# Second attention of a two-layer block: chunks of 512 tokens, parts copied inside SBUF, maxima added by a selection product

## What is computed

```python
qkv = (x @ W_qkv).reshape(B, S, 3, H, Dh)            # H = 16 heads of Dh = 8
q, k, v = (q[:, :, m], k[:, :, m], v[:, :, m])       # m: a fixed permutation of the tokens
qs = q.reshape(B, H, nseg, seg, Dh)                  # segments of 128 tokens
ks = k.reshape(B, H, nseg, seg, Dh)[:, :, :, ::dil]  # every second key: 64 per segment
scores = jnp.einsum('bhnqd,bhnkd->bhnqk', qs, ks) * scale
attn = jax.nn.softmax(scores, axis=-1)
out = jnp.einsum('bhnqk,bhnkd->bhnqd', attn, vs)
```

## Time and profile before

| | |
|---|---|
| median of three runs | 799.55 us |
| the profiled execution, its own time | 806.35 us |
| its span, first to last instruction | 804.5 us |
| mean granted TensorE clock | 0.915 |
| first attention, first to last unit | about 28.6 to 372 us |
| second attention, first `seg_max` to last weighted sum | 422.4 to 480.9 us |
| expert work begins | 522.4 us |

### The profile page before, as it was taken

One profiled execution on the slowest core, in us unless ns is written; L12 is line 12 of the kernel. 1 busy time (PEld: TensorE's weight loads), 2 busy tenths in 40 slices (PEclk: granted clock), 3 DMA queues, 4 the chain that ended last, 5 costly groups with the idle time before them and its releaser, 6 DMA issues.

```text
span 804.5 us, 16665 instructions
## 1 busy us (share of the span) xinstructions
PE 689.3 (86%) x5878; PEld 441.6 (55%) x5878; DVE 636.0 (79%) x1149; ACT 445.1 (55%) x974; POOL 155.7 (19%) x287
## 2 busy tenths in 40 slices
PE   7499888888888888899955988499999998998883
PEld 5233333333333333335533766499999997996652
DVE  2688999999999999942574647889999994554996
ACT  3058999999999999984641436202111114454442
POOL 6400000000000000003331007601111122123563
PEclk9558999999999999999985669589999998999998
DMA  7711111111111110002556500000000000000000
GB/s 197 222 22 32 32 32 31 32 32 31 33 31 32 32 31 3 2 3 68 142 140 172 156 16 1 0 1 0 2 0 0 0 0 1 0 0 1 15 13 26
DMA packets 19401, 31.87 MB, mean 40 GB/s; under 512 B 4952, under 2 KB 12504, under 8 KB 18040
## 3 DMA queue, kind: packets, MB, share of 16 engines
q1 hardware_dynamic: 17992, 29.42, 13.9%
q0 software_dynamic: 1344, 1.58, 0.7%
HBM read 23.25 MB, written 7.34 MB: 38 GB/s over the span
## 4 chain that ended last, share of the span: by engine, by line
PE 52%; ACT 18%; issue 10%; DVE 10%; DMA 5%; SPq 2%; POOL 2%; DVEq 0%; POOLq 0%; ACTq 0%
ACT probs L1166 16%; PE ps_hi L749 13%; PE ps_lo L998 7%; PE ps_lo L1000 6%; PE ps_lo L999 6%; PE ps_hi L763 4%; PE ps_hi L1058 3%; DMA q_rep<-mrow 2%; DVE probs L1747 2%; DVE mx L1465 2%; PE ps_hi L1049 1%; SPq L385 1%; ACT mrow L1121 1%; PE ps_hi L810 1%; PE ps_hi L930 1%
## 5 line engine op out<-in xcount | busy, mean ns | idle before, releaser
L1465 DVE TENSOR_REDUCE mx<-ps_lo 128x2 f32<-128x1024 f32 x256 | 306.2, 1224 | 12.2 <-PE ps_lo L726 9.0
L1166 ACT ACTIVATE probs<-ps_hi 128x512 f32<-128x512 f32 x512 | 278.0, 596 | 38.4 <-PE ps_hi L749 25.8
L763 PE MATMUL ps_hi<-probs,v_blk 128*32 128x256 f32 x2048 | 168.2, 401 | 5.6 <-ACT mrow L1121 5.5
L749 PE MATMUL ps_hi<-q,k 28*128 28x512 f32 x512 | 132.0, 509 | 26.9 <-ACT probs L1166 13.0
L726 PE MATMUL ps_lo<-k,q 26*128 26x512 f32 x512 | 135.7, 526 | 7.0 <-DVE mx L1465 4.2
L1681 DVE SCALAR_TENSOR_TENSOR tok_cur<-ps_lo,w_cur,tok_cur 128x384 f32<-128x384 f32 x240 | 127.6, 608 | 6.3 <-PE ps_lo L1000 4.7
L749 PEld LDWEIGHTS ps_hi<-q,k 28*128 28x128 f32 x512 | 49.5, 187 | 139.5 <-ACT probs L1166 117.7
L998 PE MATMUL ps_lo<-w_hi,op_hi 128*128 128x384 f32 (+1 forms) x304 | 108.1, 356 | 19.8 <-DVEq L1642 10.1
L999 PE MATMUL ps_lo<-w_lo,op_hi 128*128 128x384 f32 (+1 forms) x304 | 105.4, 347 | 0.0
L1000 PE MATMUL ps_lo<-w_hi,op_lo 128*128 128x384 f32 (+1 forms) x304 | 105.4, 347 | 0.0
L763 PEld LDWEIGHTS ps_hi<-probs,v_blk 128*32 128x32 f32 x2048 | 42.3, 109 | 72.5 <-ACT probs L1166 58.5
(11 more groups left out here) (225 smaller groups left out, 842.8 us busy)
## 6 DMA issues: line engine op xcount, KB each, us to landing
q<-q_parts SPq DMA_DIRECT2D x30, 192.0 KB
q_rep<-q_parts SPq DMA_DIRECT2D x8, 576.0 KB
k<-k_parts SPq DMA_DIRECT2D x32, 96.0 KB
k_rep<-k_parts SPq DMA_DIRECT2D x24, 96.0 KB
q_parts<-qk_hi SPq DMA_DIRECT2D x8, 256.0 KB, 4.9
q_parts<-qk_p SPq DMA_DIRECT2D x12, 128.0 KB, 3.1
xa<-in_L_attn_x SPq DMA_DIRECT2D x4, 256.0 KB, 3.9
q_parts<-qk_lo SPq DMA_DIRECT2D x4, 256.0 KB, 6.3
```

The costliest lines, as they stand in the source:

```text
L749: mm = pe.matmul(bank(4 + (2 * n + a) % 3), k0[rows, k_at:k_at + P], q0[rows, h * QN:(h + 1) * QN], start=True, stop=True)
L763: mm = pe.matmul(o_bank()[32 * r:32 * r + 32, 0:OW], v_all[:, at:at + 32], probs0[:, n % P_RING, r * OW:(r + 1) * OW], start=(kb == 0), st ...
L1166: act.activation(probs0[:, n % P_RING, a * QN:(a + 1) * QN], bank(4 + (2 * n + a) % 3), ACT.Exp).then_inc(s0_free, 1)
L1465: dve.reduce_max(mx2[:, j % 2, :, i, kh], bank(2 * (m % 2), 2).rearrange("p (a n) -> p a n", a=2), AX_X).then_inc(max0_done, 1)
```

## The change

Work is ordered by chunk instead of by batch entry: a step is now one chunk of 512 tokens (four segments) and eight of the sixteen heads, in two row strips of 64 partitions, one for even and one for odd heads. Only six pairs of parts are kept, 48 rows per strip, without the pairs (1, 2), (2, 1) and (2, 2). The way through DRAM goes: SyncE copies q (`load_q1`) and GpSimd copies k (`load_k1`) straight from the split parts, 12 DMAs each per chunk, 96 in all. For this the channels of q and k must lie in another order, which is made by permuting the weights: they are loaded into a staging tile and GpSimd copies them into place, at the start of the program, ahead of its work for head 0. The maxima are no longer two rows of q: after each head's four score products two products with a constant 0/1 matrix (`sel_sb`, 256 KB, loaded with the weights) add them. `seg_rows` gets a second product, `seg_o` moves from VectorE to ScalarE, and the transposes back are two per tile.

```diff
-ROWS = PARTS * PARTS * DH
+PART_PAIRS = ((0, 0), (0, 1), (0, 2), (1, 0), (1, 1), (2, 0))
+ROWS = len(PART_PAIRS) * DH
+HALF = 64
+HP = H // 2
+KN = QN // 2
...
-    dq1 = nc.dram_tensor("q_parts_1", [PARTS * DH, NH, S], BF16).ap()
-    dk1 = nc.dram_tensor("k_parts_1", [PARTS * DH, NH, S // 2], BF16).ap()
...
+        w_stage = attT[:, 0, 0:2 * D]
+        def copies_of(part, side):
+            return [i for i, pair in enumerate(PART_PAIRS) if pair[side] == part]
+        def copy_rows(strip, i):
+            return slice(HALF * strip + i, HALF * strip + ROWS, len(PART_PAIRS))
...
-            def store_q1(q):
...
-            def stored1(b):
...
-            def load_rep(s):
-                slot, n = s % RING, S * HG // 2
-                sp.dma_start(q_rep[0:ROWS, slot * HG * S:(slot + 1) * HG * S],
-                             dq1[:, s * HG:(s + 1) * HG].rearrange("r h n -> r (h n)").unsqueeze(1).broadcast_to(
-                                 [PARTS * DH, PARTS, HG * S])).then_inc(rep1_in[slot], 16)
...
-            def load_mrow(s):
-                at = (s % RING) * (HG * S)
-                sp.wait_ge(mrow_set, s + 1)
-                for part in range(2):
-                    dst = q_rep[MAX_ROW + part:MAX_ROW + part + 1, at:at + HG * S]
-                    sp.dma_start(dst.rearrange("o (r n) -> o r n", n=P), mrow[:, part, :]).then_inc(mrow_in, 16)
+            def load_q1(q):
+                for part in range(PARTS):
+                    sp.wait_ge(part_set[part], q + 1)
+                    for i in copies_of(part, 0):
+                        for strip in range(2):
+                            sp.dma_start(q_rep[copy_rows(strip, i), q * HP * QN:(q + 1) * HP * QN]
+                                         .rearrange("d (h n) -> d h n", n=QN),
+                                         qk_p[HALF * strip:HALF * (strip + 1), q, part, 0:QN]).then_inc(q1_in[q], 16)
...
-            for dst, src in ((wo_sb, wo), (w_qkv1, w_qkv), (wout_sb, w_out), (sim_sb, sim), (rank_sb, rank)):
+            for dst, src in ((wo_sb, wo), (wout_sb, w_out), (sim_sb, sim), (rank_sb, rank)):
                 sp.dma_start(dst[:], src).then_inc(ld_w1, 16)
+            sp.dma_start(w_qkv1[:, 2 * D:W3], w_qkv[:, 2 * D:W3]).then_inc(ld_w1, 16)
+            sp.dma_start(w_stage, w_qkv[:, 0:2 * D]).then_inc(ld_w1, 16)
+            sp.dma_start(sel_sb[:], sel).then_inc(ld_w1, 16)
...
-            for q in range(2):
-                store_q1(q)
-            stored1(0)
-            sp.wait_ge(const_set, 12)
+            sp.wait_ge(const_set, 11)
             sp.wait_ge(s0_ps, NU)
-            for s in range(2):
-                load_rep(s)
-            for q in range(2, NQ):
-                store_q1(q)
-            load_mrow(0)
-            for s in range(2, RING):
-                load_rep(s)
-            load_mrow(1)
-            stored1(1)
-            for s in range(NS - RING):
-                sp.wait_ge(seg_s_ps, 2 * (s + 1))
-                load_rep(s + RING)
-                load_mrow(s + 2)
-            for s in range(NS - RING + 2, NS):
-                load_mrow(s)
+            for q in range(NQ):
+                load_q1(q)
...
+            def load_k1(q):
+                for part in range(PARTS):
+                    pool.wait_ge(part_set[part], q + 1)
+                    for i in copies_of(part, 1):
+                        for strip in range(2):
+                            pool.dma_start(k_rep1[copy_rows(strip, i), q * HP * KN:(q + 1) * HP * KN]
+                                           .rearrange("d (h n) -> d h n", n=KN),
+                                           qk_p[HALF * strip:HALF * (strip + 1), q, part, QN:QN + KN]
+                                           ).then_inc(k1_in[q], 16)
...
+            pool.wait_ge(ld_w1, 7 * 16)
+            for n in range(2):
+                at = slice(n * D, (n + 1) * D)
+                pool.tensor_copy(w_qkv1[:, at].rearrange("p (s d h) -> p h s d", s=2, d=DH),
+                                 w_stage[:, at].rearrange("p (h s d) -> p h s d", s=2, d=DH)).then_inc(w1_set, 1)
...
-            fill(k_rep1[64:96, :].bitcast(words), two_ones)
...
-                for g in range(G):
-                    mm = pe.transpose(bank(t % 8)[:, g * P:(g + 1) * P], source(t, g), ident_sb[:])
+                for f in range(2):
+                    mm = pe.transpose(bank(t % 8)[:, f * P:(f + 1) * P], source(t, f), ident_sb[:])
...
+            def seg_at(s, h, g):
+                at = (s // 2 * HP + s % 2 * HG + h) * QUAD + g
+                return slice(at * SEG, (at + 1) * SEG), slice(at * KSEG, (at + 1) * KSEG)
+            def seg_max(s, step):
+                n = s * (HG + 2) + step
                 if n >= 2:
-                    pe.wait_ge(seg_max_done, n - (h > 0))
...
+                    pe.wait_ge(seg_max_done, n - (step > 0))
+                rows = slice(HALF * (step % 2), HALF * (step % 2) + ROWS)
+                for h in range(2):
+                    for g in range(QUAD):
+                        q_at, k_at = seg_at(s, step // 2 * 2 + h, g)
+                        c = (h * QUAD + g) * KSEG
+                        mm = pe.matmul(bank(step % 2)[:, c:c + KSEG], q_rep[rows, q_at], k_rep1[rows, k_at],
+                                       start=True, stop=True)
                 mm.then_inc(seg_max_ps, 1)
             def seg_rows(s):
                 pe.wait_ge(seg_max_all, s + 1)
-                pe.transpose(bank(0)[0:STEPS, 0:P], mx[:], ident_sb[:]).then_inc(seg_max_ps, 2)
+                pe.transpose(bank(0)[0:STEPS, 0:P], mx[:], ident_sb[:])
+                pe.matmul(bank(0)[STEPS:2 * STEPS, 0:P], mx[:], ident_sb[:], start=True, stop=True,
+                          tile_position=(0, STEPS)).then_inc(seg_max_ps, 2)
             def seg_scores(s, f):
-                slot = s % RING
-                pe.wait_ge(mrow_in, 32 * (s + 1))
+                pe.wait_ge(mrow_set, s + 1)
                 if s:
                     pe.wait_ge(seg_s_free, 2 * s - 1 + f)
-                for g in range(4 * f, 4 * f + 4):
-                    for h in range(HG):
...
+                for h in range(HG):
+                    def dst(u):
+                        return bank(2 + 2 * f, 2)[:, (u * HG + h) * SEG:(u * HG + h + 1) * SEG]
+                    for u, strip in ((0, 0), (1, 1), (1, 0), (0, 1)):
+                        q_at, k_at = seg_at(s, h, 2 * f + u)
+                        rows = slice(HALF * strip, HALF * strip + ROWS)
+                        pe.matmul(dst(u)[HALF * strip:HALF * (strip + 1)], k_rep1[rows, k_at], q_rep[rows, q_at],
+                                  start=True, stop=True, tile_position=(HALF * strip, HALF * strip))
+                    for u in range(2):
+                        at = ((2 * f + u) * HG + h) * P
+                        mm = pe.matmul(dst(u), sel_sb[:, at:at + P], mrow[:, s % 2, :], start=False, stop=True,
+                                       skip_group_check=True)
                 mm.then_inc(seg_s_ps, 1)
             def seg_out(s):
...
                 pe.wait_ge(seg_s_free, 2 * s + 2)
                 if s >= 2:
                     pe.wait_ge(seg_o_free, s - 1)
...
+                for g in range(QUAD):
+                    for h in range(HG):
+                        at = (s % 2) * 2 * S + (g * HG + h) * SEG
+                        mm = pe.matmul(bank(6 + s % 2)[32 * h:32 * h + 32, g * SEG:(g + 1) * SEG],
+                                       vblk(s // 2 * QUAD + g, s % 2 * HG + h), probs[:, 0, at:at + SEG],
+                                       start=True, stop=True, tile_position=(0, 32 * h))
...
-                pe.wait_ge(rep1_in[s % RING], (1 + PARTS) * 16 * (s // RING + 1))
+                if s % 2 == 0:
+                    pe.wait_ge(q1_in[s // 2], 2 * len(PART_PAIRS) * 16)
+                    pe.wait_ge(k1_in[s // 2], 2 * len(PART_PAIRS) * 16)
...
+            def seg_o(s):
+                act.wait_ge(seg_p_free, s + 1)
+                copy(o_seg[:, s * QN:(s + 1) * QN], bank(6 + s % 2)).then_inc(seg_o_free, 1)
...
-                if s:
-                    dve.wait_ge(mrow_in, 32 * s)
-                dve.tensor_scalar(mrow[:, 0, :], bank(0)[0:STEPS, 0:P], -1.0, None, ALU.mult).then_inc(seg_max_done, 1)
+                if s >= 2:
+                    dve.wait_ge(seg_s_ps, 2 * (s - 1))
+                low = slice(STEPS, 2 * STEPS)
+                dve.tensor_scalar(mrow[:, s % 2, :], bank(0)[0:2 * STEPS, 0:P], -1.0, None, ALU.mult).then_inc(
+                    seg_max_done, 1)
                 dve.wait_ge(seg_max_done, n + 1)
...
+                dve.scalar_tensor_tensor(out=mrow[low, s % 2, :], in0=bank(0)[low, 0:P], scalar=-1.0,
+                                         in1=mrow[low, s % 2, :], op0=ALU.mult, op1=ALU.subtract).then_inc(
+                                             seg_max_done, 1)
...
-            def seg_o(s):
-                dve.wait_ge(seg_p_free, s + 1)
```

(37 more changed lines are left out.)

90 lines of the change are left out of this document (16 added, 74 removed).

## The result

The changed kernel takes **822.73 us** (median of six runs, 819.11 to 828.97), the kernel before 802.44 us in the same comparison (six runs, 799.33 to 807.79): ratio 1.0294, 95% interval 1.0257 to 1.0331. It is slower by 20 us where 8 were forecast, and it lies beyond the range's upper end of 816. The profiled execution took 826.42 us, 20.07 more than the one of before.

The account below looks back on a forecast made before the run. Transfers were taken to bound the second attention's start and middle, TensorE the rest. Second attention's start -4.7, loop +13.3 and -7.0, program start +6.7 make +8.3 us on the median of 799.55: 807.8 us, range 788 to 816.

Parts of the forecast that it names:

- Start of the second attention: Before the second attention's loop: without the way through DRAM, reductions start at 418.3 instead of 423.1, a gain of 4.7 us.
- The root of the router: Behind 48 issues, it would be there at 435.2 us, VectorE asking at about 438: cost nothing, 3 us of cover.
- Start of the program: GpSimd waits for all seven weight loads before head 0, so `mx_parts` begins 6.7 us late and nothing gives it back.
- The loop, price of a step: Second attention's loop: 8.54 us per step at half clock, 63.0 us in all against 49.7, so 13.3 us more.
- a change of mode: Within a loop step: each of 16 changes between two-strip and full-width products costs 0.017 us, 0.27 per step.
- the drains: Rival (8%): up to 0.107 us per change of mode in the loop, 12 us more over 128 changes, about 820 us.
- A selection product: Each of 16 `sel_sb` products per loop step takes 0.107 us at half clock, 1.71 us per step.
- The loop, share of full clock: The loop keeps the earlier trace's 10.9 us at full clock, which saves 7.0 us.
- The rival "full clock from the third step": Rival (18%): TensorE reaches full clock from the loop's third step on; loop 43.5 us, time 795.4 us.
- Transposes and `seg_o`: Half the transposes back and `seg_o` on ScalarE were counted at nothing; without VectorE's cover the transposes would win some 4 us.

Follow-up runs that it names:

- copies later: The changed kernel with GpSimd's wait for the weight loads and its two copies moved behind the maxima of the fifth head: 818.59 us, ratio 1.0165.
- grouped: The changed kernel with all 16 score products of a half-step first, then its 8 selection products: 801.03 us, ratio 1.0009.
- one-mode: The changed kernel with maxima and selection matrix on both strips, each selection product split into two 64x64 ones: 803.94 us, ratio 1.0022.
- three repaired starts: GpSimd's copies behind the fifth head, SyncE's loads after the first head's maxima row: on the changed kernel 812.02 us, with products grouped 792.67, with two-strip 64x64 products 789.25.
- interleaved: Products grouped and GpSimd's copies late, plus the 16 maxima products of two steps alternating between the two row strips: 793.26 us, ratio 0.9896.
- grouped one with late copies: The changed kernel with 16 score then 8 selection products per half-step and GpSimd's two copies behind the fifth head: 795.51 us, ratio 0.9922.

## Why the prediction was wrong, and where it was right

- **Start of the second attention: right.** 3.9 of 4.7 us. SyncE took 0.68 per copy, GpSimd 0.59, its copies landed in 2.6, and none was waited for. The root of the router ran at 438.6 to 441.5 and held nobody.
- **Start of the program: right on the term, short on its tail.** 6.8 against 6.7 us at `mx_parts`. Called a loss that nothing gives back, and so it was; but moving GpSimd's wait alone would not have undone it, since `mx_parts` hides a DMA queue that is filled by the same loads.
- **The loop, price of a step: this is the step that failed.** I took 0.017 us for a change of mode from a unit of the first attention and gave the drains 8%. It is 0.124. A us at full clock saves 0.5: the loop is 70.5 us with 3.5 of them, 66.85 with 10.7 (copies later). So it is 72.2 all at half clock, where 63.0 was forecast. The 9.2 missed are found again in the starts. A group of four scores and two selection products takes 0.675 where the terms make 0.498: 64 of them are +11.3. (Two changes cost 0.214 more than I took; the scores beside them 0.037 less, since my 0.062 apiece, from the earlier trace rows, already had a change in it.) The last pair before maxima products has none behind it (-0.135 x 12 = -1.6), the maxima products are cheaper since their strips partly overlap (-0.18 x 12 = -2.2), `seg_rows` is dearer (+0.12 x 6 = +0.7), and TensorE waits 1.2 us in the first step: together +9.4. A selection product itself is 0.107, as forecast.
- **Why the wrong row.** The 0.017 was no price of a change; it came from a wrong count of columns. I took the unit's four row-strip products two at a time, 1024 columns or 0.853 us. The timeline of TensorE before has the four start together:

```profile
54.14 0.79 PE L749 MATMUL ps_hi<-q,k 28*128 28x512 f32 x2
54.14 0.79 PE L726 MATMUL ps_lo<-k,q 26*128 26x512 f32 x2
54.87 1.08 PE L763 MATMUL ps_hi<-probs,v_blk 128*32 128x256 f32 x8
55.88 0.79 PE L749 MATMUL ps_hi<-q,k 28*128 28x512 f32 x2
```

The weighted sums follow after 0.73 us, less than the 0.853 I gave them. Side by side on four strips they have 512 columns, 0.427 us (an estimate), which leaves 0.30; and the weighted sums take 1.01, 0.16 over their own 0.853. So this row left room for two changes after all, and the earlier trace rows had one in each group: scores 0.147 over their columns, maxima 0.107. The Trainium skill (TensorEngine Tiling (Array Packing), Key Properties) says that changing the mode drains the engine; the grouped and one-mode kernels agree that a change costs time, 0.14 and 0.124 us, though no row shows what the engine does in it. The rival's own 0.107, from the earlier trace rows, was within 15%. Its 820 us was nearest to the result, short of it by the clock.

- **The loop, share of full clock: about right on its length, wrong on its worth and its cause.** I kept 10.9 us. The profiled execution had 3.5, in one stretch; three other traces with 16 changes had some 10.7 each, in three short stretches. They save 1.7 and 5.3 us where I took 7.0, since a change costs nearly the same at either clock. What I did not see is that mode changes and clock go together. With 16 changes the clock is full for 3.5 to 10.7 us (four traces), with 8 for 23.9 (one), with 4 for 27 to 28 (five) and once 17.6; without selection products for 22.5 of 37.5. What links the two stays open: a drained array as the reason is argued, not shown, for the trace has TensorE busy throughout, and the 17.6 show that the number of changes alone does not set it.
- **The rival "full clock from the third step"** came true in loop length, 42.4 against 43.5 us, once 12 of the 16 changes were gone.
- **Transposes and `seg_o`: nothing, as forecast.** 9.7 us from the loop's end to the projection's first product against 10.0.

## What to carry to other kernels

Price a change of tiling mode per pair of tile shapes, from products of just these shapes, and order products so that one shape runs as long as PSUM allows: here the order alone is worth some 22 us, half of it or more through the clock as far as the loops tell. Check the columns you give a row against its start-to-start times, group by group, before taking a price from the rest of a sum. When an engine that serves the critical path is given a wait for a load, look also at which small DMA now stands behind that load. A TensorE that reads 100% busy may still lose time at changes of tile: compare its start-to-start times with its columns before trusting it.

## What the runs showed of the hardware

- A change between 64x64 and 64x128 tiles costs 0.124 us at clock 0.50 and 0.11 at 1.00, nearly the same time at half the speed. Selection products followed by maxima products, both of full width on a 64-row strip, show none (two in 0.19 us).
- Four 32-row strips run side by side in the first attention: four products start together (54.14), and the weighted sums follow after 0.73 us at half clock. Two 64-row strips run side by side for scores and for selections: four products of 128 columns take 0.213 us at 1.2 GHz. Maxima products, alternated between strips, go from 0.46 to 0.34 us for 16 at full clock.
- A step was 9.44 of 9.44 us busy at 0.50. The same products in another order ran at 1.00 for 28 of 42 us.
- When the clock rises in the first attention varies: before 60 us in the three repaired starts, in the interleaved and in the one without selection products; at 60 in the grouped one; between 66 and 78 in most others; and past 96 in the grouped one with late copies (98.9). The row below is that kernel's busy time by stage, all of it at 0.50. Its 31 head intervals took 324.1 us, in the others 307 to 316, and that execution 803.8 us against a median of 795.5. The 12 runs of that kernel go from 789.7 us at a mean clock of 0.944 to 803.8 at 0.917, so such shifts are probably a good part of the scatter between runs.

```profile
60.00:96.00 36.00, 36.00 (x253) 10.61 (x246) 25.42 (x24) 23.47 (x47) 1.92 (x8) 0.50 0.08 18
```
